# K turned by transposing DMA transfers in place of TensorE transposes, in a gated cross-attention and FFN block

## The reference

```python
def attention(x, context, Wq, Wk, Wv):      # x: (8,224,1024), context: (8,750,1024), 32 heads of 32
    q = x @ Wq.T
    kv = concat([context @ Wk.T, context @ Wv.T], -1).reshape(b, m, 32, 32, 2)
    k, v = kv[..., 0], kv[..., 1]
    q, k = rmsnorm(q), rmsnorm(k)             # over the 32 elements of a head, eps 1e-6
    attn = softmax(einsum('bhnd,bhmd->bhnm', q, k) * 32 ** -0.5)
    return einsum('bhnm,bhmd->bhnd', attn, v)

def ffn(x, w1, w2, w3):                     # w1, w2: (2816,1024), w3: (1024,2816), each rounded to -1, 0, 1
    return (sigmoid(x @ Q(w1).T) * (x @ Q(w2).T)) @ Q(w3).T

x = x + tanh(g_xattn) * attention(layernorm(x), context, Wq, Wk, Wv)
x = x + tanh(g_ffn) * ffn(layernorm(x), w1, w2, w3)
```

## Time and profile before

| | before |
|---|---|
| median of 3 runs | 2434.12 us (2430.53 to 2436.66) |
| profiled execution, its time / its span | 2427.1 / 2425.3 us |
| TensorE matmul, busy | 2369.5 us (98%) |
| VectorE busy | 1433.3 us (59%) |
| ScalarE busy | 1348.3 us (56%) |
| GpSimd busy | 854.1 us (35%) |
| DMA, mean over the span | 123 GB/s |
| mean granted TensorE clock | 0.995 |

### The profile page before, as it was taken

How to read it: one execution, slowest core, us unless ns; L and a number is a source line. 1 busy time by engine, 2 the same in 40 slices (tenths; PEclk the granted TensorE clock), 3 DMA queues, 4 the chain that set the end, 5 groups by cost and what they waited for, 6 DMA issues and landing times.

```text
span 2425.3 us, 48902 instructions
## 1 busy us (share of the span) xinstructions
PE 2369.5 (98%) x18386; PEld 1405.3 (58%) x18386; DVE 1433.3 (59%) x2537; ACT 1348.3 (56%) x2894; POOL 854.1 (35%) x857
## 2 busy tenths in 40 slices
PE   7999999999999999999999999989999999999999
PEld 5885565666666666666666666555555555544444
DVE  6666676786777777777777867664444444410000
ACT  5876787787787787887877877752111111110000
POOL 3664254564645545555545646430000000000000
PEclk9999999999999999999999999999999999999999
DMA  7785434434334443433434333453333333244351
GB/s 254 237 257 177 126 105 111 119 96 113 109 94 128 108 115 96 113 116 84 134 103 117 92 87 107 110 178 122 110 99 108 100 107 98 83 139 136 111 165 52
DMA packets 250123, 298.10 MB, mean 123 GB/s; under 512 B 110624, under 2 KB 205344, under 8 KB 249376
## 3 DMA queue, kind: packets, MB, share of 16 engines
q1 hardware_dynamic: 249888, 294.98, 41.6%
HBM read 196.22 MB, written 49.55 MB: 101 GB/s over the span
## 4 chain that ended last, share of the span: by engine, by line
PE 32%; POOL 28%; issue 28%; DMA 1%; DVE 1%; ACT 1%; POOLq 1%; SPq 0%; DVEq 0%; ACTq 0%
PE ps L1453 20%; POOL krs L705 14%; PE ps L1578 11%; POOL oinv L723 4%; POOL kms L700 3%; POOL osum L721 2%; POOL osum L728 2%; POOL ca L735 2%; POOL cn L749 1%; POOL oinv L725 1%; DMA hid<-hidden 1%; POOLq L60 0%; POOL crs L745 0%; DMA wraw<-in_wffn 0%; ACT pf L953 0%
## 5 line engine op out<-in xcount | busy, mean ns | idle before, releaser
L1485 PE MATMUL ps<-wk,cpair 128*128 128x512 f16 x4608 | 1116.8, 379 | 5.1 <-DVE cpair L1081 4.6
L1278 DVE TENSOR_TENSOR plo<-pf,phi 125x448 f16<-125x448 f32 x768 | 504.7, 658 | 203.0 <-ACT phi L944 196.7
L1485 PEld LDWEIGHTS ps<-wk,cpair 128*128 128x128 f16 x4608 | 398.8, 97 | 378.2 <-DVE cpair L1081 5.7
L953 ACT ACTIVATE pf<-ps 125x448 f32<-125x448 f32 x768 | 416.9, 543 | 244.9 <-PE ps L1505 232.8
L1453 PE MATMUL ps<-xnTh,w12q 128*128 128x512 f16 (+1 forms) x1408 | 477.6, 353 | 2.9 <-issue 2.1
L1453 PE MATMUL ps<-xnTl,w12q 128*128 128x512 f16 (+1 forms) x1408 | 477.5, 353 | 0.0
L944 ACT ACTIVATE phi<-pf 125x448 f16<-125x448 f32 x768 | 444.4, 579 | 8.5
L705 POOL TENSOR_TENSOR krs<-kms,mhalf 125x8 f32<-125x8 f32 x192 | 328.6, 1712 | 15.0
L1505 PEld LDWEIGHTS ps<-qT,kst 128*125 128x125 f16 x1536 | 208.1, 137 | 148.9 <-DMA kst<-kpair 4.2
L1529 PE MATMUL ps<-val,phi 125*128 125x65 f16 x3072 | 279.0, 192 | 12.0 <-DVE plo L1278 11.8
L700 POOL TENSOR_TENSOR kms<-kss,keps 125x8 f32<-125x8 f32 x192 | 72.3, 376 | 616.5 <-DVE kss L1233 616.5
(11 more groups left out here) (115 smaller groups left out, 2653.2 us busy)
## 6 DMA issues: line engine op xcount, KB each, us to landing
gbuf<-in_wffn SPq DMA_DIRECT2D x66, 512.0 KB, 4.8
wraw<-in_wffn SPq DMA_DIRECT2D x66, 512.0 KB, 5.7
kst<-kpair SPq DMA_DIRECT2D x128, 250.0 KB, 4.6
cstream<-in_ctx SPq DMA_DIRECT2D x48, 500.0 KB, 4.3
craw<-in_ctx SPq DMA_DIRECT2D x48, 500.0 KB, 5.6
hid<-hidden SPq DMA_DIRECT2D x7, 2816.0 KB, 12.7
hidden<-hh SPq DMA_DIRECT2D x66, 256.0 KB, 2.1
kst<-kpair SPq DMA_DIRECT2D x128, 125.0 KB, 2.5
```

The source lines that it names most:

```text
L953: act.activation(pf[0:KW, e % 6, :], bank(3 + e % 3)[0:KW, 0:2 * S], ACT.Exp, bias=LN128, scale=SCALE).then_inc(p_ready, 1)
L1278: dve.tensor_tensor(plo[0:KW, e % 6, :, :], pf[0:KW, e % 6, :].rearrange("p (t n) -> p t n", t=2), phi[0:KW, e % 6, :, :], ALU.subtract).t ...
L1485: mm = pe.matmul(bank(pt)[:, :], cpair[:, n % RING, a, kc, :], wkp[g][:, w, kc, :], start=(kc == 0 and m == 0), stop=(kc == KC - 1 and m = ...
```

## The change

K goes from knat to its stack in one transposing DMA transfer per tile. knat has each half twice, `[128, 2, 8 heads, 4, 32]`, so ScalarE and VectorE write 512 columns where they wrote 256, and a transposed block of 128 columns is a whole head's stack. The stack's tiles are 128 columns apart, of which 125 are used; the last three token rows of knat are cleared once, by a memset on VectorE ahead of the attention stage. The four transposes, the copy, kpair and the eight stack transfers per unit go. `turn_k(v, tt)` waits for klo of the tile and, for tile 0, for the last scores that read the buffer. khi of tile T now waits for the transfer of tile T - 2, where it waited for the transposes; the scores wait for the transfers of tiles 0 to 3 (e = 0) and of all six (e = 2).

```diff
-        kst = sb(pb, "kst", [P, 2, HG, SK], F16)
+        kst = sb(pb, "kst", [P, 2, HG, KT * P], F16)
-        knat = sb(pb, "knat", [P, 2, HG, 2, DH], F16)
+        knat = sb(pb, "knat", [P, 2, HG, 4, DH], F16)
-        kpair = sb(pb, "kpair", [P, NP, SK], F16)
...
-            def stack_k(v, part):
-                t0, t1 = ((0, 4), (4, KT))[part]
-                sp.wait_ge(kpair_ready, v * KT + t1)
-                if v >= 2:
+            def turn_k(v, tt):
+                T = v * KT + tt
+                sp.wait_ge(klo_ready, T + 1)
+                if tt == 0 and v >= 2:
                     sp.wait_ge(s_ready, (v - 1) * NQ)
-                for i in range(2):
-                    for s in range(2):
-                        sp.dma_start(kst[HD2 * i:HD2 * i + HD2, v % 2, s:HG:2, KW * t0:KW * t1],
-                                     kpair[HD2 * s:HD2 * s + HD2, :, KW * t0:KW * t1]
-                                     ).then_inc(kst_in[v % 2][part], 16)
+                sp.dma_start_transpose(kst[:, v % 2, :, P * tt:P * tt + P],
+                                       knat[:, T % 2, :, :, :].rearrange("p h a d -> p (h a d)")).then_inc(kt_in[T % 2], 16)
...
                         load_qT(u, par, b, g)
+                        for tt in range(4):
+                            turn_k(u, tt)
...
-                        stack_k(u - 1, 0)
+                        turn_k(u - 1, 4)
                         if g == G - 1 and b < B - 1:
                             load_ctx((b + 1) * KT + 3)
-                        stack_k(u - 1, 1)
+                        turn_k(u - 1, 5)
...
                             load_ctx((b + 1) * KT + 4)
+                        turn_k(u, 0)
                         load_qT(u, par, b, g)
...
                             load_ctx((b + 1) * KT + 5)
+                        turn_k(u, 1)
+                        turn_k(u, 2)
                         if g == 1 and b >= 1:
                             x1_save(2 * b - 2)
                             x1_save(2 * b - 1)
                         if g == 2 and b >= 1:
                             cn_save(2 * b - 1)
+                        turn_k(u, 3)
                 if k == U:
-                    stack_k(U - 1, 0)
-                    stack_k(U - 1, 1)
+                    turn_k(U - 1, 4)
+                    turn_k(U - 1, 5)
...
-                        wait(act, kT_ready, Tb - 1)
-                        act.activation(knat[0:KW, pt, :, 0, :], khat[0:KW, :, :], ACT.Copy).then_inc(khi_ready, 1)
+                        if Tb == 0:
+                            act.wait_ge(knat_clear, 1)
+                        wait(act, kt_in[Tb % 2], 16 * (Tb // 2))
+                        act.activation(knat[0:KW, pt, :, 0::2, :], khat[0:KW, :, :].unsqueeze(2).to_broadcast([KW, HG, 2, DH]),
+                                       ACT.Copy).then_inc(khi_ready, 1)
...
             half_low(2 * NT - 1, 1)
+            dve.memset(knat[:, :, :, :, :], 0.0).then_inc(knat_clear, 1)
...
-                        dve.tensor_tensor(knat[0:KW, 1 - pt, :, 1, :], khat[0:KW, :, :],
-                                          knat[0:KW, 1 - pt, :, 0, :], ALU.subtract).then_inc(klo_ready, 1)
+                        dve.tensor_tensor(knat[0:KW, 1 - pt, :, 1::2, :],
+                                          khat[0:KW, :, :].unsqueeze(2).to_broadcast([KW, HG, 2, DH]),
+                                          knat[0:KW, 1 - pt, :, 0::2, :], ALU.subtract).then_inc(klo_ready, 1)
...
-                        dve.wait_ge(kT_ready, Tb)
-                        if v >= 1:
-                            dve.wait_ge(kst_in[1 - kp][tt // 4], 64 * ((v - 1) // 2 + 1))
-                        dve.tensor_copy(kpair[:, :, tt * KW:tt * KW + KW],
-                                        bank(2, F16).rearrange("p (h n) -> p h n", n=P)[:, 0:NP, 0:KW]
-                                        ).then_inc(kpair_ready, 1)
...
-                            pe.wait_ge(kst_in[ap][e // 2], 64 * ((u - 1) // 2 + 1))
+                            v = u - 1 if e >= 0 else u - 2
+                            for i in range(2):
+                                pe.wait_ge(kt_in[i], 16 * (KT // 2 * v + 2 + e // 2))
...
-                                           kst[:, ap, hd, KW * kt:KW * kt + KW], qT[:, ap, hd, :],
+                                           kst[:, ap, hd, P * kt:P * kt + KW], qT[:, ap, hd, :],
...
-                        pe.wait_ge(klo_ready, T - 1)
-                        wait(pe, kpair_ready, T - 2)
-                        for h in range(NP):
-                            mm = pe.transpose(bank(2, F16)[:, h * P:h * P + KW],
-                                              knat[0:KW, pn, 2 * h:2 * h + 2, :, :].rearrange("p h a d -> p (h a d)"),
-                                              identh[0:KW, 0:KW])
-                        mm.then_inc(kT_ready, 1)
```

More of the change, by code:

```diff
@@ L227, in flamingo_kernel @@
         q_in = [sem(f"q_in{i}") for i in range(2)]
-        kst_in = [[sem(f"kst_in{i}_{h}") for h in range(2)] for i in range(2)]
+        kt_in = [sem(f"kt_in{i}") for i in range(2)]; knat_clear = sem("knat_clear")
         pad_ready = sem("pad_ready")
@@ L233, in flamingo_kernel @@
         krs_ready = sem("krs_ready"); khat_ready = sem("khat_ready"); khi_ready = sem("khi_ready")
-        klo_ready = sem("klo_ready"); kT_ready = sem("kT_ready"); kpair_ready = sem("kpair_ready")
+        klo_ready = sem("klo_ready")
         v1_ready = sem("v1_ready")
@@ L1250, in unit_b @@
                             op0=ALU.mult, op1=ALU.mult).then_inc(khat_ready, 1)
-                    if j == 2 and behind(k, t, 2):
-                        tt = (t - 2) % KT
-                        kp = par if t >= 2 else 1 - par
-                        v = u if t >= 2 else u - 1
-                        dve.wait_ge(kT_ready, Tb)
-                        if v >= 1:
-                            dve.wait_ge(kst_in[1 - kp][tt // 4], 64 * ((v - 1) // 2 + 1))
-                        dve.tensor_copy(kpair[:, :, tt * KW:tt * KW + KW],
-                                        bank(2, F16).rearrange("p (h n) -> p h n", n=P)[:, 0:NP, 0:KW]
-                                        ).then_inc(kpair_ready, 1)
                     if w_late(u) and r == 4 * W_B_SUM[u] + 2:
@@ L1425, in x_half @@
                     pe.wait_ge(stage_in[i % 3], 16 * (i // 3 + 1))
-                if h == 0:
-                    pe.wait_ge(kpair_ready, KT * U)
                 if h == 1:
@@ L1536, in unit_b @@
                     if j == 1 and behind(k, t, 2):
-                        pn = pt
-                        pe.wait_ge(klo_ready, T - 1)
-                        wait(pe, kpair_ready, T - 2)
                         if w_late(u) and t == W_B_SUM[u]:
                             w_sum(w_late(u), bank(2)[:, 256:256 + WQ])
-                        if w_late(u) and t == W_B_SUM[u] + 1:
-                            pe.wait_ge(wfr_step, 2 * w_late(u) + 1)
-                        for h in range(NP):
-                            mm = pe.transpose(bank(2, F16)[:, h * P:h * P + KW],
-                                              knat[0:KW, pn, 2 * h:2 * h + 2, :, :].rearrange("p h a d -> p (h a d)"),
-                                              identh[0:KW, 0:KW])
-                        mm.then_inc(kT_ready, 1)
                     q = tail_step(k, r)
```

## The result

The changed kernel takes 2407.38 us, the median of 4 runs (2405.68 to 2409.68), against 2432.98 us before (4 runs, 2430.53 to 2436.66). The ratio is 0.9895, with a 95% interval of 0.9882 to 0.9908: 25.6 us faster, where 36.2 had been forecast (2398 us). Its profiled execution took 2409.68 us (span 2407.9), the slowest of its four. That of before took 2427.1, about 6 us under its median.

A forecast was written before the change was run, and what follows sets the result against it. TensorE paces the attention stage; -41.3 + 1.7 + 3 + 1.7 - 3.3 + 2 = -36.2 us, giving 2390.9 us profiled and 2398 us as median. Its own range was 2388 to 2410; the wider range, leaving out 2 in 10, 2386 to 2580.

The forecast's parts named there:

- TensorE's price is the difference of two rounds, not 73.3 us of busy time.: Attention stage: removing four K transposes saves TensorE 0.215 us a tile, 41.3 us over 192 tiles.
- Not returned: 1.7 and 3 us in the first unit and units 1 to 4.: Where TensorE is not the pacer: 1.7 us lost in first unit and drain, 3 us written off in units 1 to 4.
- The memset costs 1.7 us.: Start of attention stage: new 2048-column memset delays the first context split by 1.7 us, bounds 0 and 2.5 us.
- The gates are held up, at no cost.: SyncE's queue: K pieces hold up the Q load, gates and context loads; no separate term for gates in the sum.
- VectorE ends 0.15 us a tile lighter, ScalarE is covered.: K split at 512 columns, copy gone: VectorE -0.15 us a tile; ScalarE +0.22 us, hidden under TensorE at 85% busy.
- Rival (c): ScalarE paces: its added 0.22 us shows in half the tiles, gain 20 us, 2414 us; chance 0.08 shared with part of (b).
- The wait for the last unit's stack, 3.3 us, goes.: Last unit: TensorE's 3.29 us wait for the K stack goes, its last piece being sent six rounds ahead, not four.
- Engine time D 3.5 us, landing 4.5 us.: Each transposing K transfer holds the DMA engines 3.5 us and lands 4.5 us after issue; engines at 76%.
- Late pieces, 2 us.: Attention stage: K pieces landing late behind bursts of loads cost 2 us.
- Rival (a): DMA engines become the bound from 5.36 us a transfer; 2556 us at 6, 2993 us at 8.3; chance 0.25.
- Rival (b): Late landing at unit handover, third score: 1.2 us each gives about 2434 us, chance 0.07 for all given back; 2414 in part.

The follow-up runs named there:

- one transpose of four: Kernel before with three of the four K transposes of each tile left out from unit 4 on, copy, stack transfers and waits kept: 2408.90 us, ratio 0.9894.
- Repairing it: Changed kernel with each unit's first two gate loads issued ahead of its first K transfer and Q loads: 2396.04 us, ratio 0.9852.
- The kernel with two copies: Changed kernel with each K transfer sent twice from unit 2 on, splits and scores waiting for both: 2418.64 us, ratio 0.9941.
- narrow halves: Changed kernel with both halves of the K split written at 256 columns, not 512, leaving out some score products: 2392.69 us, ratio 0.9832.

## Why the prediction was right, and where it was not

The direction and the main mechanism were right: TensorE paces the stage, and its time came back where nothing else was late. 2407.38 us lies in both ranges given, but only 2.6 us inside the forecast's upper end of 2410, and the gain was 25.6 us of 36.2. The side costs were too small in sum, and the width of the range, more than their working, kept the result inside. By the steps:

- *TensorE's price is the difference of two rounds, not 73.3 us of busy time.* Right, and returned in full: 1.34 us a unit wherever nothing else is late, 0.223 us a tile against 0.215. For 192 tiles that is 42.9 us. The run with one transpose of four shows it without the rest of the change.
- *Not returned: 1.7 and 3 us in the first unit and units 1 to 4.* Too careful for units 1 to 3, which gave 4.52 us. Unit 4 had the gates. (Unit 0 holds four tiles' transposes, not six, 0.4 us less.)
- *The memset costs 1.7 us.* The instruction took 0.91 us and made TensorE's wait 1.07 us longer. Unit 0 took 4.55 us more in these two profiles and some 3 us more in the means, with more time at half clock. Moving the memset gave 2.2 us back in one pair of profiles and 1.9 in another.
- *The gates are held up, at no cost.* This step of the working failed. I named them among what stands behind the first K transfer and gave them no term. What was missing is not the transfer in front of them but the faster rounds: a gate block that goes out some 20 us after its unit's start does not move when TensorE does. The kernel before showed its gate sums 4.4 and 3.7 us after their issue in units 4 and 5, against some 9.8 us in the median; that row was there to be read. In units 4 to 7 the forecast gain of 5.2 us became a loss of 0.5, and with one transpose of four, and the old queue, a gain of 3.9 became a loss of 0.2. In unit 31 a gain of 1.3 became a loss of 0.7; there the kernel with one transpose of four stalls for 0.6 us and the changed one for 2.0, so the K transfer ahead of the gates has a part. Repairing it gave 10.1 us, 2.4 of them stalls of the kernel before.
- *VectorE ends 0.15 us a tile lighter, ScalarE is covered.* The durations came out as the Q split's rows said (684 and 629 ns), and the net was beside the point. The wider subtract stands where khat and GpSimd's inverse root are waited for, and the copy that left did not help there. Measured: 6.1 us in units 8 to 30, and ScalarE's share 1.5. This is the second term put at nothing. Rival (c) named the wrong engine, and by its own terms its time is about 2419 us, since 21 us less of the 36.2 leave 15.
- *The wait for the last unit's stack, 3.3 us, goes.* It went, and the drain still took 50.7 us in both. In the drain TensorE's waits for P rose from 4.8 to 6.8 us, and its mean granted clock was 0.82 where it had been 0.90 (1541.8 to 1592.5 and 1561.0 to 1611.8 us). How much each took back is not separated; drains of the other profiles take 48.7 to 52.4 us.
- *Engine time D 3.5 us, landing 4.5 us.* Too high: 0.20 more share for one more transfer a tile of 6.85 us is 1.4 us, against 1.8 by the step from 0.40 to 0.50. The kernel with two copies has 190,080 more packets for 16 x (0.575 x 2413.0 - 0.468 x 2407.9) = 4170 us of engine time, 21.9 ns a packet. I had used the mean of all packets, 64.6 ns, which are 4.6 times as large. Neither number changed the outcome, since the bound was far.
- *Late pieces, 2 us.* None in steady units: a landing took 3.1 us in the median, 8.9 at the worst, of a cover of 10.7.

By the Trainium skill ("DMA: Bandwidth & Descriptors", Latency and other measured facts) 261 GB/s, given there for a non-contiguous middle dimension, would make D an estimated 1.0 us; the runs show 262 KB in 1.4 to 1.8 us, 145 to 190 GB/s. The 1309 ns that the Trainium skill gives for one block ("VectorE: DVE Perf Modes", The three transpose paths) are not a price per block in a larger transfer: eight blocks landed in 3.1 us.

Rival (a) did not happen, and its point was real: it lies between two and three transfers a tile. Rival (b), waits at the third score, was nowhere. Outside the attention stage the two profiles differ by 4.2 us in the wrong direction (2.4 before it, 1.8 after), and the medians differ by 4.0 us more than the stage does. A part of this goes with the clock. The first K and V matmul starts at 203.4 and 203.6 us in the two profiles without a half-speed stretch near 31 us, at 204.2 to 205.3 in the eight with one of 3.4 us (the kernel before among them), and at 205.8 to 206.6 in the four with 6.8 us (the changed kernel among them). The tail took 814.5 to 815.1 us in eleven profiles and 815.7, 816.4 (the changed kernel) and 817.3 in three. And times go with the clock over whole executions: at a mean granted clock of 0.995 or 0.996 the kernel before took 2427.1 (its profiled execution) to 2430.1 us (four executions), at 0.991 or 0.992 2433.3 to 2436.3 (five). Why the clock differs between executions of one kernel stays open. So does the 0.4 us that g = 2 loses with narrow halves.

## What to carry to other kernels

Where one engine paces a stage strictly, price an instruction on it by the distance between its neighbours' starts, and expect it back in full; then look for the losses in the rounds that carry rare side work, not in the averages. When a change makes that engine faster, list the transfers whose time is set by something else, with the margin that the trace shows between issue and use: the ones with the smallest margin become the bound, whether or not the change touches their queue. Move ahead of a waiting entry whatever has its buffer free already. And before a few us at the start or the end of a stage are put down to an edit, compare profiles of kernels that are alike there.

## What the runs showed of the hardware

- A transposing transfer of 128 x 1024 two-byte elements from SBUF to SBUF: issue 1.23 us (1232 ns at the least, 1234 in the median, 3625 at the most), landing 3.0 us at the least and 3.1 in the median, 1.4 to 1.8 us of all 16 engines, some 1,056 packets. The strided stack copies that it replaced took 590 to 1940 ns of issue each.
- A VectorE operation can be held by a long one of GpSimd. In a unit with g = 2 of the changed kernel:

```profile
1138.88 2.13 POOL L751 TENSOR_TENSOR cn<-ca,cn 128x1024 f16<-128x1024 f32 x1
1138.94 0.42 DVE L1254 SCALAR_TENSOR_TENSOR khat<-ps,krs 125x256 f32<-125x256 f32 x1 [0.36 <-POOL krs L707]
1139.29 2.74 DVE L1274 TENSOR_TENSOR plo<-pf,phi 125x448 f16<-125x448 f32 x2
```

Two subtracts of 0.62 us took 2.74 us, the first of them 2.20; it ended 0.48 us after GpSimd's subtract. In all 14 places of the changed kernel where the two meet, VectorE's subtract took 2.08 to 2.21 us and ended those 0.48 us behind GpSimd's. khat, which reads PSUM, was not held (0.42 us). The other way about, GpSimd's add of 0.19 us took 1.22 us in the rows of the K split above, while VectorE ran an operation of 1.26 us; that the one held the other is not shown.
- Near the start of the stage TensorE's granted clock fell to half for 3.4 or 6.8 us, with waits of 1.7 to 4.5 us there. Longer waits went with more time at half (the memset paragraph), but the instructions alone don't fix it: profiles of kernels that start alike show none, 3.4 or 6.8 us at half near 31 us, and differ by 1.1 to 1.6 us in unit 0.
